# Moving the experts' weight loads and the last tiles' routing steps in a hand-written schedule (layers of scan, mixture of experts, attention and MLP, one Trainium2 core)

## The chip, the core and the metric

The kernel runs on 1 core of one Trainium2 (trn2) chip. The metric is the device time of one execution in microseconds (us). Five engines run their own instruction streams and meet at semaphores: TensorE (PE in the rows, PEld for its weight loads), VectorE (DVE), ScalarE (ACT), GpSimd (POOL) and SyncE (SP). SP computes nothing: it waits for semaphores and issues DMAs one after the other (SPq in the rows).

## What is computed

Input x is [2, 1024, 256] in f32, that is 2048 tokens of 256 channels. Four residual layers follow each other:

```
x = x + scan_layer(layernorm(x))      # state-space scan, 64 states per channel, sequential over 1024 tokens
x = x + moe(layernorm(x))             # 8 experts, top 2, capacity 640 tokens an expert
x = x + linear_attention(layernorm(x))
x = x + gated_mlp(layernorm(x))
```

The part that matters here is the end of the first and the beginning of the second. The scan layer ends per token with `(y + x*D_param) @ out_proj_w.T`, and its sum with x is the residual x1. The mixture layer begins with

```
probs = softmax(layernorm(x1) @ Wg)
gate_vals, expert_idx = top_k(probs, 2)
pos = running count of the tokens, in token order, that chose the same expert
dispatched = rows of layernorm(x1), laid out by (expert, pos), where pos < 640
h = relu(dispatched @ w1[e]);  out = h @ w2[e]
```

A token's place depends on all tokens before it, so the tiles are ranked in order. An expert's rows may come from any tile.

## The kernel before, in words

Tokens are cut into 16 tiles of 128 (tiles 0 to 15), and for the scan into 32 chunks of 64 (two chunks a tile). `prepare` makes the scan's inputs, `selective_scan` runs the scan and everything up to the dispatch of the tokens, `experts` the eight experts, `second_layer` the attention and the MLP.

The order of the work in `selective_scan` is one list of steps, made by the generator `scan_schedule`. Every engine walks through the same list and picks the steps in which it has a part; the order of the list is thus the order in every engine's queue, SP's too. Semaphores do the rest, so a step stands still on an engine while the step ahead of it waits.

For each group of 16 channels of a chunk ("stream"), PE makes the factors and inputs, ACT the exponentials, DVE one long scan instruction (L1161). Behind the scan of a chunk come:

- "y": PE multiplies the states by C (L945). "y_out": ACT copies the result to the tile y_raw (L1098).
- "y_sel", the pick: SP issues 4 DMAs of 16 KB each that gather the wanted partitions of y_raw into the tile y_sb (L867). It waits for the chunk's "y_out". The last chunk, 31, has no pick: PE selects its rows itself, by 4 products (L984).
- "yT": PE turns both chunks of the tile (L980 from y_sb, and L984), and waits for the pick to have landed. "yt": ACT copies them to y_t (L1107, L1108) and POOL adds the skip term (L1332). "proj", "proj2": PE multiplies by the output weights (L956). "resid": DVE adds the input (L1185, tile x1o), and SP stores the rows (L860, x1_d).

Routing goes by blocks of tiles: (0 to 3), (4 to 7), (8 to 11), then b3 = tiles 12 to 14 and b4 = tile 15 alone. The steps of a block are NORM (stats L1203, aggr L1208, the square root on ACT L1114, the reciprocal L1212, norm L1219, and a copy of the token numbers L1223), "turn" (PE transposes the normed rows, L1007), "turned" (ACT copies them to the tile r_xt, L1125), "score" (PE, the gate's weights, L1017), CHOOSE ("logit" L1227, "top" L1240, "index" L1245, "sub" L1248, "exp" on ACT L1132, "float" L1252, "hot" L1255, "ind" L1259), "rank" (PE counts by products with a triangle, L1030 to L1034), WEIGH (L1262 to L1268), SETTLE (L1272 to L1292; "slot" writes the tile slots), "count", and "scatter": POOL issues two indirect DMAs a tile that write the normed rows to their places in disp_d (L1339). ACT's L1116, right behind the square root of b4, is a load of the table for Exp and a small activation that brings it forward.

"load_experts" is one more step, of SP alone: when the last inputs of the scan are made it issues the loads of w1 and w2 of experts 0 and 1, 4 DMAs of 1 MB (L889), into the tile `shared`, which held the scan's factors until then. In the kernel before it stands in the list at the last stream step, that is ahead of the last residual of the loop, the last pick (chunk 30), and the whole tail.

Then SP waits for the stores of x1 and for all 32 scatters, and `experts` begins: SP loads the rows of experts 0 and 1 from disp_d (L1512, xd), then everything for the second layer (L1560, L1562); PE transposes the rows (L1400) and multiplies (L1412, L1424).

The two lines that hold the waits of which most is said later:

```
sp.wait_ge(sem("y_out"), c + 1)                       # the pick, on SP
pe.wait_ge(sem(f"y_sel{th}"), Y_SEL * (c + 1))        # "yT", on PE
```

Of the kernel before, what the change touches and what calls it, by code (L numbers as in the profile page):

```python
# [630 lines left out]
TOTAL = CHUNKS * GROUPS  # L631
# [9 lines left out]
ROUTED = ((0, 4), (4, 4), (8, 4), (12, 3), (15, 1))  # L641
# [3 lines left out]
CHOOSE = ("logit", "top", "index", "sub", "exp", "float", "hot", "ind")  # L645
WEIGH = ("sum", "inv", "gate")
SETTLE = ("pick", "where", "kept", "slot")


def router_steps(blk):  # L650

    n = ROUTED[blk][1]
    yield from ([(name,)] for name in NORM)
    for i in range(n):
        yield ([("mm", i - 1)] if i else []) + [("tr", i)]
        yield [("xt", i)]
    yield [("mm_last", n - 1)]
    yield from ([(name,)] for name in (*CHOOSE, *WEIGH, "rank", *SETTLE, "count"))
    for i in range(n):
        for j in range(2):  # L660
            yield [("scatter", i, j)]
# [7 lines left out]
def scan_schedule():  # L669

    routing, z, open_z, ending = [], 0, False, False

    def stamp(name, *args):
        nonlocal z, open_z
        if name in Z_WRITE:
            assert not open_z
            open_z = True
            return (name, *args, z)  # L680
        if name in Z_DONE:
            open_z, z = False, z + 1
            return (name, *args, z - 1)
        if name in ("mm", "proj2"):
            return (name, *args, z)
        return (name, *args)

    def advance(c=CHUNKS, j=5):
        if routing:
            blk, steps = routing[0]  # L690
            if any(name in Z_WRITE for name, *args in steps[0]) and (ending or open_z or j not in ((5,), (1, 3))[c % 2]):
                return
            for name, *args in steps.pop(0):
                yield stamp(name, blk, *args)
            if not steps:
                routing.pop(0)

    def finish(i, what):

        nonlocal ending  # L700
        if what == "yT":
            ending = True
        yield stamp(what, i)
        if what == "resid":
            ending = False
            if i + 2 < TILES:
                yield ("load_epilogue", i + 2)
            for b, (first, n) in enumerate(ROUTED[:-2]):
                if i == first + n - 1:
                    routing.append((b, list(router_steps(b))))  # L710

    for gi in range(TOTAL + LAG):
        c, j = divmod(gi, GROUPS)
        if gi < TOTAL:
            starts = j == 0 and c % CPB
            yield ("stream", gi)
            if starts:
                yield stamp("first_out", c)
        elif gi < TOTAL + LAG:
            yield ("scan", gi - LAG)  # L720
        yield from advance(c, j)
        if c >= CHUNKS - 4 and routing and not any(name in AT_PACE for name, *args in routing[0][1][0]):
            yield from advance(c, j)
        c_read, step = divmod(gi - LAG, GROUPS)
        c_read -= 1
        if 0 <= c_read < CHUNKS and step < len(Y_STEPS) and Y_STEPS[step]:
            yield ("y", c_read, Y_STEPS[step])
        for at, what in ((Y_OUT, "y_out"), (Y_PICK, "y_sel")):
            ended, rest = divmod(gi - LAG - GROUPS - at, GROUPS)
            if rest == 0 and 0 <= ended < CHUNKS - 1:  # L730
                yield (what, ended)
        for at, at_last, what in TILE_END:
            for i in range(TILES - 1):
                if gi == GROUPS * (CT * (i + 1)) + LAG + Y_OUT + (at if i < TILES - 2 else at_last):
                    yield from finish(i, what)
        if j == GROUPS - 1 and (c + 1) % CPB and c + 1 < CHUNKS:
            yield stamp("first", c + 1)
        if j < len(LOADS) and 1 <= c < CHUNKS - 1:
            yield ("load_parts", c + 1, j)
        if gi == GROUPS + 2:  # L740
            yield from (("load_epilogue", 0), ("load_weights",))
        if gi == 2 * GROUPS + 2:
            yield ("load_epilogue", 1)
        if j == GROUPS // 2 and 4 <= c < 4 + 2 * ZEROS:
            yield ("zero_slots", c - 4)
        if gi == TOTAL - 1:
            yield ("load_experts",)
    while routing:
        yield from advance()


    b3, b4 = len(ROUTED) - 2, len(ROUTED) - 1
    yield ("y_sel", CHUNKS - 2)
    yield from ((name, b3) for name in NORM)
    for js in (js for js in Y_STEPS if js):
        yield ("y", CHUNKS - 1, js)
    yield ("y_out", CHUNKS - 1)
    yield stamp("yT", TILES - 1)
    yield ("turn", b3)
    yield stamp("yt", TILES - 1)  # L760
    yield ("turned", b3)
    yield stamp("proj", TILES - 1)
    yield stamp("proj2", TILES - 1)
    yield from (("score", b3, i) for i in range(ROUTED[b3][1]))
    yield stamp("resid", TILES - 1)
    yield from ((name, b4) for name in NORM)
    yield from (("turn", b4), ("turned", b4), ("score", b4, 0))
    yield from ((name, b3) for name in CHOOSE)
    yield ("rank", b3)
    yield from ((name, b4) for name in CHOOSE[:-1])  # L770
    yield from ((name, b3) for name in WEIGH)
    yield from ((name, b3) for name in (*SETTLE, "count"))
    yield from (("scatter", b3, i, j) for i in range(ROUTED[b3][1]) for j in range(2))
    yield (CHOOSE[-1], b4)
    yield ("rank", b4)
    yield from ((name, b4) for name in (*WEIGH, *SETTLE))
    yield from (("scatter", b4, i, j) for i in range(ROUTED[b4][1]) for j in range(2))


def selective_scan(k, a, s):  # L780
    pe, act, dve, pool, sp, sem = k.pe, k.act, k.dve, k.pool, k.sp, k.sem
    ident, eps, slots = s["ident"], s["eps"], s["slots"]
    with ExitStack() as ctx:
# [29 lines left out]
        bank_in = [k.psum[:, 1024:2048], k.psum[:, 2048:3072]]  # L813
        bank_y, bank_z = k.banks[6], k.banks[7]
        schedule = list(scan_schedule())
        x1_at = {c: z + 1 for kind, *x in schedule if kind == "resid" for c, z in (x,)}
        u0_at = {c: z + 1 for kind, *x in schedule if kind == "first_out" for c, z in (x,)}
# [1187 lines left out]
```

## Time and profile before

| | us |
|---|---|
| 3 runs of the kernel before, median | 1322.31 |
| lowest and highest of the three | 1314.65, 1324.99 |
| the profiled execution, its own time | 1319.23 |
| its span, from first to last instruction | 1317.8 |
| mean granted clock of TensorE in it, as a share of full | 0.924 |
| busy: PE, DVE, ACT, POOL | 1105.0, 842.5, 503.4, 306.7 |

All rows come from the profiled execution; its own time is 1.4 us longer than its span. Times in the rows are counted from the start of the span. The scan ends at about 691 us, the dispatch lasts until about 727 us, the experts run from 732 to about 1025 us, and the second layer ends the span. The busy shares are averages over these very different stages.

### The profile page before, as it was taken

Reading aid. Unit: us, or ns where it says so; the run is one execution under the profiler, and the core shown is the slowest. Engines: PE = TensorE matmul, PEld = TensorE weight load, DVE = VectorE, ACT = ScalarE, POOL = GpSimd, SP = SyncE. Lnnn points to the kernel's source line nnn. Section 1 sums busy time; section 2 is a strip of 40 time slices with the busy share of each in tenths; the row PEclk is TensorE's granted clock in tenths of the full one; section 3 lists DMA queues with packets and bytes.
Section 4 is the critical chain, followed back from the end, with each engine's and each line's share of the span. In section 5 each row is a group of like instructions: output and inputs, shape, how many; then the busy total and the mean of one; then the engine's idle time right before and its main releaser. Section 6 shows DMA issues by size and latency. Waiting matters only on the chain.

```text
span 1317.8 us, 29499 instructions
## 1 busy us (share of the span) xinstructions
PE 1105.0 (84%) x11952; PEld 701.6 (53%) x11952; DVE 842.5 (64%) x1006; ACT 503.4 (38%) x1245; POOL 306.7 (23%) x930
## 2 busy tenths in 40 slices
PE   3647888878878898888873799999999588999998
PEld 2435444444544454444432578888887245475565
DVE  5858999999999999999992111111211577742211
ACT  3865556566656655566551111111111110122110
POOL 9741222222233222522242011111111200000000
PEclk9865789999999899999996799999999698999999
DMA  3897345543222222322223823222200400000000
GB/s 107 243 281 215 77 96 132 131 118 82 57 62 76 55 60 52 82 57 49 53 70 148 313 79 102 100 101 99 80 16 16 128 0 0 0 9 8 16 16 16
DMA packets 171687, 112.02 MB, mean 85 GB/s; under 512 B 93637, under 2 KB 162248, under 8 KB 169248
## 3 DMA queue, kind: packets, MB, share of 16 engines
q1 hardware_dynamic: 163120, 88.69, 24.2%
q0 software_dynamic: 8000, 20.87, 4.8%
q8 instruction: 94, 1.54, 0.5%
q10 hardware_dynamic: 432, 0.59, 0.2%
q14 instruction: 41, 0.34, 0.1%
HBM read 63.18 MB, written 45.90 MB: 83 GB/s over the span
## 4 chain that ended last, share of the span: by engine, by line
PE 47%; DVE 27%; issue 14%; SPq 5%; ACT 4%; DMA 2%; POOL 1%; DVEq 0%; ACTq 0%; POOLq 0%
DVE h L1161 19%; PE psum L1412 11%; PE psum L1424 11%; PE psum L1896 8%; PE psum L1907 4%; PE psum L945 3%; DVE den L1726 2%; PE psum L931 2%; PE psum L1852 2%; ACT decay L1046 1%; PE psum L912 1%; SPq L278 1%; SPq L199 1%; PE psum L1844 1%; SPq L282 1%
## 5 line engine op out<-in xcount | busy, mean ns | idle before, releaser
L1161 DVE TENSOR_TENSOR_SCAN h<-decay,psum 128x1024 f32<-128x1024 f32 x256 | 565.8, 2268 | 14.8 <-ACT psum L1056 9.0
L1046 ACT ACTIVATE decay<-psum 128x512 f32<-128x512 f32 x512 | 279.2, 600 | 200.5 <-PE psum L912 197.9
L931 PE MATMUL psum<-xdiag,bstat 96*128 96x64 bf16 x4096 | 176.4, 200 | 56.2 <-DVE h L1161 53.4
L931 PEld LDWEIGHTS psum<-xdiag,bstat 96*128 96x128 bf16 x4096 | 144.9, 102 | 82.0 <-DVE h L1161 73.5
L912 PEld LDWEIGHTS psum<-rows,shared 32*128 32x128 bf16 x4096 | 79.0, 96 | 183.4 <-issue 119.9
L945 PE MATMUL psum<-h,cstat 128*32 128x512 f32 x1024 | 150.2, 664 | 1.1 <-DVE h L1161 1.1
L1412 PE MATMUL psum<-xdt,shared 128*128 128x320 f32 x512 | 141.0, 436 | 0.7 <-ACT xdt L1471 0.7
L1424 PE MATMUL psum<-shared,hid 128*128 128x256 f32 x640 | 139.5, 379 | 0.6 <-ACT hid L1465 0.6
L1317 POOL TENSOR_TENSOR carry<-decay,h 128x16 f32<-128x16 f32 x240 | 57.9, 241 | 343.7 <-ACT decay L1046 343.4
L1424 PEld LDWEIGHTS psum<-shared,hid 128*128 128x128 f32 x640 | 121.0, 190 | 17.2 <-issue 1.1
L912 PE MATMUL psum<-rows,shared 32*128 32x64 bf16 x4096 | 110.5, 195 | 15.7 <-ACT decay L1046 7.4
L1412 PEld LDWEIGHTS psum<-xdt,shared 128*128 128x128 f32 x512 | 98.3, 192 | 41.4 <-issue 2.2
L1896 PE MATMUL psum<-xt,wgu 128*128 128x512 f32 x256 | 112.8, 600 | 2.5 <-DVE at L1731 2.5
L1499 DVE TENSOR_SCALAR hid<-psum 128x320 f32<-128x320 f32 x64 | 31.5, 492 | 112.2 <-PE psum L1412 112.2
L1534 POOL DMA_INDIRECT picked_d<-eo,to x40 | 39.0, 975 | 258.8 <-ACT eo L1468 133.5
L899 PE MATMUL psum<-r_tri 128*128 128x512 bf16 x222 | 67.8, 387 | 28.8 <-ACT decay L1046 27.5
L1502 DVE TENSOR_SCALAR eo<-psum,gate 128x256 f32<-128x256 f32 x20 | 9.7, 484 | 116.9 <-PE psum L1424 111.1
L1896 PEld LDWEIGHTS psum<-xt,wgu 128*128 128x128 f32 x256 | 49.1, 192 | 64.2 <-issue 59.4
L1749 DVE TENSOR_TENSOR shared<-psum,sil 128x512 f32<-128x512 f32 x32 | 22.1, 692 | 81.4 <-PE psum L1896 81.4
L1465 ACT ACTIVATE hid<-psum 128x320 f32<-128x320 f32 x64 | 28.0, 437 | 118.4 <-PE psum L1412 118.4
L1820 ACT ACTIVATE sil<-psum 128x512 f32<-128x512 f32 x32 | 19.1, 597 | 131.2 <-PE psum L1896 127.1
L1323 POOL TENSOR_TENSOR carry<-carry,u 128x16 f32<-128x16 f32 x240 | 52.8, 220 | 24.5 <-ACT u L1084 4.2
(201 smaller groups left out, 1100.9 us busy)
## 6 DMA issues: line engine op xcount, KB each, us to landing
shared<-in_w SPq DMA_DIRECT2D x16, 1024.0 KB, 4.8
xdiag<-x_parts_d SPq DMA_DIRECT2D x256, 48.0 KB
x_parts_d<-x_parts POOLq DMA_DIRECT2D x46, 256.0 KB, 7.8
parts_d<-dt_parts SPq DMA_DIRECT2D x24, 256.0 KB, 8.4
rows<-parts_d SPq DMA_DIRECT2D x128, 48.0 KB
disp_d<-zero SPq DMA_DIRECT2D x4, 1305.0 KB, 8.5
xd<-disp_d SPq DMA_DIRECT2D x8, 652.5 KB, 6.4
picked_d<-zero SPq DMA_DIRECT2D x4, 1024.0 KB, 5.2
```

The source lines that it names most:

```text
L899: pe.q.matmul(bank, tri[:, 1, :], tri[:, 1, :].unsqueeze(1).broadcast_to([P, 4, P]), start=True, stop=True)
L912: ins = pe.q.matmul(bank_a[half][:, i * T:(i + 1) * T], s["astat"][strip, RCH * g + q, :], rows[strip, c % 2, q, :], start=True, stop=True)
L931: ins = pe.q.matmul(to.rearrange("p d (s e) -> p s d e", e=2), bstat[0:ROWS, c % 2, b, :], xdiag[0:ROWS, c % 2, b, :, d, :], start=True, s ...
L945: ins = pe.q.matmul(bank_y[32 * q:32 * q + 32, :].rearrange("p (s d e) -> p s d e", s=2, e=4), s["cstat"][:, tok // 4, :], h[:, first:last ...
L1046: act.q.activation(decay[:, gi % NB, 8 * half:8 * half + 8, :], per_d(bank_a[half]), ACT.Exp).then_inc(sem("exp"), 1)
L1161: dve.q.tensor_tensor_scan(out=h[:, half_slot(c, half), ch:ch + G, :].rearrange("p d t -> p (d t)"), data0=decay[:, gi % NB, :, :].rearran ...
L1317: pool.q.tensor_tensor(whole, first, h[:, half_slot(c - 1, half), ch:ch + G, T - 1], ALU.mult).then_inc(sem("carry_made"), 1)
L1323: pool.q.tensor_tensor(whole.rearrange("p (h i) -> p h i", h=2), whole.rearrange("p (h i) -> p h i", h=2), own, ALU.add).then_inc(sem("car ...
L1412: ins = pe.q.matmul(table.bank(key)[:, 0:half_cap], w1[:, e % 2, dh, f * P:(f + 1) * P], xdt[:, e % 2, dh, c * half_cap:(c + 1) * half_cap ...
L1424: ins = pe.q.matmul(table.bank(key)[:, 0:D], hid[:, e % 2, f, st * P:(st + 1) * P], w2[:, e % 2, f, :], start=f == 0, stop=f == FT - 1)
L1896: ins = pe.q.matmul(table.bank(key)[:, :], wgu[:, j, dh, f * P:(f + 1) * P], xt[:, u, dh, :], start=dh == 0, stop=dh == 1)
L1907: ins = pe.q.matmul(table.bank(key)[:, 0:D], gt[:, blk % 2, f, n * P:(n + 1) * P], wd[:, f, :], start=f == 0, stop=f == FT - 1)
```

## The change

`load_experts` leaves the last stream step and is put behind the last pick, `y_sel` of chunk 30. In the tail, b3's turn goes ahead of tile 15's "yT", its scores ahead of tile 15's projection, and its CHOOSE (all but the exponential) and rank ahead of tile 15's residual and of b4's NORM. The exponential of b3 stands behind b4's NORM, and so behind the table load. All of b4's CHOOSE stands behind b3's scatter steps; before, all but its last step stood ahead of b3's WEIGH.

```diff
-        if gi == TOTAL - 1:
-            yield ("load_experts",)
     while routing:
         yield from advance()
 
 
     b3, b4 = len(ROUTED) - 2, len(ROUTED) - 1
     yield ("y_sel", CHUNKS - 2)
+    yield ("load_experts",)
     yield from ((name, b3) for name in NORM)
     for js in (js for js in Y_STEPS if js):
         yield ("y", CHUNKS - 1, js)
+    yield ("turn", b3)
     yield ("y_out", CHUNKS - 1)
+    yield ("turned", b3)
     yield stamp("yT", TILES - 1)
-    yield ("turn", b3)
     yield stamp("yt", TILES - 1)
-    yield ("turned", b3)
+    yield from (("score", b3, i) for i in range(ROUTED[b3][1]))
     yield stamp("proj", TILES - 1)
     yield stamp("proj2", TILES - 1)
-    yield from (("score", b3, i) for i in range(ROUTED[b3][1]))
+    yield from ((name, b3) for name in CHOOSE if name != "exp")
+    yield ("rank", b3)
     yield stamp("resid", TILES - 1)
     yield from ((name, b4) for name in NORM)
+    yield ("exp", b3)
     yield from (("turn", b4), ("turned", b4), ("score", b4, 0))
-    yield from ((name, b3) for name in CHOOSE)
-    yield ("rank", b3)
-    yield from ((name, b4) for name in CHOOSE[:-1])
-    yield from ((name, b3) for name in WEIGH)
-    yield from ((name, b3) for name in (*SETTLE, "count"))
+    yield from ((name, b3) for name in (*WEIGH, *SETTLE, "count"))
     yield from (("scatter", b3, i, j) for i in range(ROUTED[b3][1]) for j in range(2))
-    yield (CHOOSE[-1], b4)
+    yield from ((name, b4) for name in CHOOSE)
     yield ("rank", b4)
```

The two lines that go shift everything below them in the changed file, so that a line number there is 2 lower than in the kernel before (L867 is L865).

SP's queue at the end of the scan, in the kernel before. y_sb is the pick, shared<-in_w the experts' weights, x_d<-x1o the store of a tile's residual, xd<-disp_d the experts' rows:

```order
L867 DMA y_sb<-y_raw 32x128 x4
L889 DMA shared<-in_w 128x2048 x4
L860 DMA x_d<-x1o 128x256
L867 DMA y_sb<-y_raw 32x128 x4
L860 DMA x_d<-x1o 128x256
L1512 DMA xd<-disp_d 128x5x261 x2
```

The same place of SP's queue in the changed kernel:

```order
L865 DMA y_sb<-y_raw 32x128 x4
L858 DMA x_d<-x1o 128x256
L865 DMA y_sb<-y_raw 32x128 x4
L887 DMA shared<-in_w 128x2048 x4
L858 DMA x_d<-x1o 128x256
L1510 DMA xd<-disp_d 128x5x261 x2
```

The 4 weight loads have gone from ahead of tile 14's store and the last pick to behind both.

PE's queue behind the last states, in the kernel before (h,cstat is "y"; ident,y_sb and ident,y_raw are "yT"; ident,decay is "turn", since the normed rows of b3 and b4 lie in the tile decay; w_out,y_t the projection; r_wg,r_xt the scores; r_ind and r_before the rank):

```order
L945 MATMUL psum<-h,cstat 32x512 x20
L980 MATMUL psum<-ident,y_sb 128x128
L984 MATMUL psum<-ident,y_raw 128x32 x4
L1007 MATMUL psum<-ident,decay 128x128 x6
L956 MATMUL psum<-w_out,y_t 128x256 x2
L1017 MATMUL psum<-r_wg,r_xt 128x8 x6
L1007 MATMUL psum<-ident,decay 128x128 x2
L1017 MATMUL psum<-r_wg,r_xt 128x8 x2
L1030 MATMUL psum<-r_ind,r_tri 128x24
```

The same place of PE's queue in the changed kernel:

```order
L943 MATMUL psum<-h,cstat 32x512 x20
L1005 MATMUL psum<-ident,decay 128x128 x6
L978 MATMUL psum<-ident,y_sb 128x128
L982 MATMUL psum<-ident,y_raw 128x32 x4
L1015 MATMUL psum<-r_wg,r_xt 128x8 x6
L954 MATMUL psum<-w_out,y_t 128x256 x2
L1028 MATMUL psum<-r_ind,r_tri 128x24
L1030 MATMUL psum<-r_ind,r_tri 128x16
L1030 MATMUL psum<-r_ind,r_tri 128x8
L1032 MATMUL psum<-r_before,r_tri 128x24
L1005 MATMUL psum<-ident,decay 128x128 x2
L1015 MATMUL psum<-r_wg,r_xt 128x8 x2
```

The 6 transposes of b3 are now ahead of the wait for the pick, the 6 scores ahead of the projection, and b3's rank ahead of b4's transposes. On ACT, b3's three copies to r_xt stand ahead of the two to y_t, and its exponential is the first instruction behind the table load and its small activation. On DVE, b3's eight steps from L1227 to L1259 stand ahead of tile 15's residual and norm, and b4's stand behind b3's count. POOL's queue is the same. The number of instructions, of table loads and of DMAs is the same on every engine.

## Rows read from the trace of the kernel before

**Rows 1.** Chain of waits in order of time, 693 to 735 us: start us, us, what.

```profile
693.99 9.08 DMA y_sb<-y_raw
...
703.21 0.45 PE psum L980
...
708.44 0.43 DVE x1o L1185
...
709.89 1.28 ACT L1116
...
716.07 0.33 POOL disp_d L1339
...
725.06 2.46 DMA disp_d<-decay,slots
...
727.89 4.11 DMA xd<-disp_d
...
732.05 2.20 PE psum L1400 x9
```

**Rows 2.** Timeline of SP's queue: start us, us, engine, line, op, out<-in, count.

```profile
687.84 2.09 SPq L889 DMA_DIRECT2D shared<-in_w  x4
691.75 0.33 SPq L860 DMA_DIRECT2D x_d<-x1o  x1
692.17 2.44 SPq L867 DMA_DIRECT2D y_sb<-y_raw  x4
...
728.88 0.52 SPq L1560 DMA_DIRECT2D x<-x_d  x1
```

**Rows 3.** DMA issues of two stretches: count, KB each, us to landing.

```profile
x_d<-x1o SPq DMA_DIRECT2D x1, 128.0 KB, 1.7
...
skip_c<-skip_d SPq DMA_DIRECT2D x1, 128.0 KB, 2.6
```

**Rows 4.** Stretches: us, busy PE, PEld, DVE, ACT, POOL, clock, DMA share, GB/s.

```profile
696.00:697.00 1.00, 0.00 (x0) 0.00 (x0) 0.00 (x0) 0.00 (x0) 0.00 (x0) 1.00 1.10 460
698.00:699.00 1.00, 0.00 (x0) 0.00 (x0) 0.00 (x0) 0.00 (x0) 0.00 (x0) 0.50 1.01 426
701.00:702.00 1.00, 0.00 (x0) 0.00 (x0) 0.00 (x0) 0.00 (x0) 0.00 (x0) 0.50 0.57 182
...
738.00:740.00 2.00, 2.00 (x8) 1.37 (x7) 0.49 (x1) 0.05 (x1) 0.00 (x0) 0.80 1.12 370
```

**Rows 5.** Timeline of the engines, 688 to 717 us, columns as in rows 2.

```profile
688.28 1.13 PE L956 MATMUL psum<-w_out,y_t 128*128 128x256 f32 x4 [0.53 <-POOL y_t L1332]
691.46 3.64 PE L945 MATMUL psum<-h,cstat 128*32 128x512 f32 x32 [1.05 <-DVE h L1161]
695.17 0.77 ACT L1098 COPY y_raw<-psum 128x128 f32<-128x128 f32 x4 [1.65 <-PE psum L945]
...
705.01 1.52 PE L1007 MATMUL psum<-ident,decay 128*128 128x128 f32 x6
706.53 1.87 PE L956 MATMUL psum<-w_out,y_t 128*128 128x256 f32 x4
708.24 1.40 PE L1017 MATMUL psum<-r_wg,r_xt 128*128 128x8 f32 x12
...
705.24 0.27 ACT L1107 COPY y_t<-psum 128x128 f32<-128x128 f32 x1 [9.29 <-PE psum L984]
706.57 0.92 ACT L1125 COPY r_xt<-psum 128x256 f32<-128x256 f32 x3 [0.90 <-PE psum L1007]
711.29 0.35 ACT L1125 COPY r_xt<-psum 128x256 f32<-128x256 f32 x1
...
710.49 0.17 DVE L1227 COPY r_logit<-psum 128x24 f32<-128x24 f32 x1
712.03 0.18 DVE L1259 TENSOR_TENSOR r_ind<-r_hot 128x24 bf16<-128x24 f32 x1
713.73 0.17 DVE L1262 TENSOR_REDUCE r_total<-r_prob 128x3 f32<-128x24 f32 x1
```

## The prediction

> **What bounds the kernel now.** I read the page first (its busy shares mix stages, so they decide nothing here), then the chain of waits in order of time around the end of the scan, then SP's queue and the stretches of the same time, then the timeline of the engines for the prices. In the chain [rows 1] the reader is to see four pieces. From 693.99 us the chain is a DMA, the last pick, for 9.08 us: it lands at 703.07 and PE starts "yT" at 703.21. From there to 716.07 it runs through PE, ACT and DVE in many small steps: tile 15's residual, its norm, and both blocks' choosing. From 716.07 to 725.06 it is POOL, that issues the eight scatters of b3 and b4. Then fixed latencies: 2.46 us until the last scatter has landed, the issue of the experts' rows at 727.89, 4.11 us until they are there, and PE begins the experts at 732.05. Nothing else is on the chain between 694 and 732, so a microsecond saved ahead of the first scatter is one saved in the whole, if nothing replaces it.
>
> Why does a pick of 4 times 16 KB take 9 us? SP's queue [rows 2] shows it: the four 1 MB loads were issued from 687.84, the pick from 692.17 to 694.61. The DMA engines are full (1.10 and 1.01 of their time, 460 and 426 GB/s at 696 and 698) and run out of work between 701 and 702, with 182 GB/s left [rows 4]. The small transfers got through only when the big ones ended. Meanwhile PE does nothing, and its granted clock, still 1.00 at 696, is 0.50 at 698 and at 701 (1.2 instead of 2.4 GHz) [rows 4]; so "yT" begins at half clock.
>
> **The change, part by part.** The sum follows the changed order from the end of "y", which it leaves where it is: PE's last L945 ends at 695.10 and ACT's copy to y_raw at 695.94 [rows 5].
>
> *The loads behind the pick.* SP waits for tile 14's residual as before and issues its store at 691.75, the pick from 692.17 [rows 2]. The four loads come behind it, from 694.6. The last of the pick's four issues begins at 693.99 [rows 1]. The trace has no pick whose landing is told and that stands free; the nearest transfers land 1.7 and 2.6 us after issue, with 128 KB each [rows 3]. So the pick is there between 695.7 and 696.6; I take 2.1 us, 696.1, in the middle. At the other end it lands no earlier than now, 703.07: that is a rival below.
>
> *Turn and "yT".* The 6 transposes took 1.52 us at half clock [rows 5]; the clock is full at that time [rows 4], so about 0.8: 695.15 to 695.95, in the time in which PE would wait for ACT and the pick anyway. They need b3's norm, which DVE made during "y". "yT" took 703.21 to 705.2 [rows 1, 5], the second of these being just ahead of ACT's copy at 705.24, at half clock; at full 1.0: 696.1 to 697.1. ACT now makes b3's three copies first, 0.92 us from 696.0 [rows 5], so to 696.95, and is free when "yT" ends. From "yT" to the start of the projection it was 705.2 to 706.53, 1.3 us over ACT and POOL: the projection can start at 698.4.
>
> *Scores ahead of the projection.* 12 passes in 1.40 us [rows 5], from 697.1, when both PE and the copies are ready: 698.5. The scores cost the projection 0.1 us only, since they run while ACT and POOL make y_t. The projection took 1.13 us at full and 1.87 at half clock [rows 5]; it ends at 699.6 or 700.4.
>
> *Choosing ahead of the residual.* From L1227 to the end of L1259 it is 710.49 to 712.21, 1.72 us [rows 5]: 698.53 to 700.25. The residual can then start at 700.28, and it would have been ready at 699.65: choosing delays tile 15's chain by some 0.6 us, and takes its own 1.72 off the end of it.
>
> *Residual to exponential.* From 708.44 [rows 1] to the first activation behind the table load at 711.29 [rows 5] it is 2.85 us, the load's 1.28 among them [rows 1]. The exponential of b3 is that activation now: 703.13. It lasts some 0.22 us, so DVE begins to weigh at 703.37. Before, b3's exponential stood behind b4's copy; now b4's copy stands behind it, 0.2 us late, which nobody needs yet.
>
> *Weighing, settling, first scatter.* From 713.73 [rows 5] to 716.07 [rows 1], 2.34 us, the same instructions and the same handing over to POOL: 705.71. Eight starts as far apart as before, 8.99 us [rows 1]: the last at 714.70. The last scatter begins 10.4 us earlier than the 725.06 of before. It needs b4's slots: all the choosing and weighing of both blocks and b4's last steps lay behind 710.49 and ended before 717, 6.5 us; even if b4 alone took all of it behind b3's count at about 705.2, its slots would stand at 711.7, and the seventh scatter (705.71 plus six of the 1.28 us between starts) comes at 713.4. So b4's choosing, moved behind b3's, is covered by POOL, with 1.7 us or more to spare.
>
> *The stretch behind it* moves as a whole. The weights: 4.2 MB at 426 GB/s [rows 4] are 9.8 us, from about 695.4, so there at 705.2, at the slow end of the stretches around 707; tile 15's store, issued at about 700.7, is queued behind them and lands by then too. SP asks for it at about 717. The experts' rows and everything behind start 10.4 us earlier, with TensorE's clock at half as now: PE has stood 16 us by 732 and has the clock back in the stretch 738 to 740 [rows 1, 4]; it will have stood nearly as long.
>
> Sum: 7.1 us from "yT" starting at 696.1 instead of 703.2, and 3.3 from the shorter way from there to the first scatter (9.6 instead of 12.9 us). 10.4 us off the profiled execution's 1319.23 is 1308.8; off the median of the three runs, 1322.31, it is 1311.9. The mean of those four executions is 1320.3, and I take 1310.
>
> Bounds of the gain: "yT" can't start before the turn and the copy to y_raw are done, 695.95, so with full clock and the pick at 695.7 it is 10.6. With half clock throughout (turn +0.7, "yT" +1.0, and scores and their copies late by half a microsecond) and the pick at 696.6, the weighing starts some 2.3 us later: 8.1. I keep 8 to 11.
>
> The row of the table load is that of two, 1.28 us, and the next activation starts directly behind it [rows 1, 5]. The Trainium skill (ScalarE: Activation LUTs, section What ACT_TABLE_LOAD costs) says that a switch costs a drain of 1.38 us on top, 2.66 in all. By that page the exponential, which now hangs directly on the load, would come 1.4 us later and the time would be 1311.4; the trace does not show such a drain, and the sum goes by the row.
>
> **Rivals.**
>
> *The pick is slow whatever stands ahead (a).* If the 16 engines serve small and big transfers that overlap alike, the pick could still land only with the weights, now issued directly behind it, at about 705.2. Turn would be early, but scores stand behind "yT" on PE, so all waits: 705.2 plus the 9.6 us from there to the first scatter is 714.8 instead of 716.07. Gain 1.3 us, time 1319. For it: the pick issued behind the weights waited 9 us. Against it: the experts' rows landed in 4.11 us although 2 MB more was issued 1 us behind them, at 728.88 [rows 1, 2]; what stands ahead wasn't held back.
>
> *Weights beside the routing (b).* The loads now run from 695 to 705, the time in which all engines route, where before they ran beside idle ones. If copies, the table load or tile 15's store suffer, say a quarter more on the 9 us from 696.1 to 705.1, 2.2 us are given back, and if the first scatters are slowed, 2 more: gain 6 to 8, time about 1313. Against it: from 688 to 696, while the loads already ran, PE went through the projection (1.13 us) and "y" (3.64 us), and ACT through its four copies (0.77 us), each back to back [rows 5].
>
> *Clock at the experts' start (c).* If PE's shorter rest left the clock at full, the 6.4 us at half from 732.05 to about 738.4 would be worth 3.2 more: gain 13.6, time 1306. Against it: PE rested from 695.1 and the clock was at half by 698 [rows 4, 5]; the rest ahead of the experts stays near 15 us.
>
> *b4 too late (d), slower.* b4's choosing behind b3's count is the one thing that gets later. It decides once its slots come behind 713.4, where the seventh scatter would start; every microsecond beyond costs one. To be at the old time they would have to come 10.4 us behind that, at 723.8, and to be 13.2 us slower than that at 737. That would be a time from 1332 on. I find 711.7 at the worst.
>
> **How the numbers follow.** Main case 0.70, (a) 0.08, (b) 0.12, (c) 0.07, (d) 0.03. One per cent, 13.2 us, is about what a measurement of this kernel can tell from no change. The forecast gain is 0.8%, inside it. The three runs lie 10 us apart, so a true 10.4 may come out above 13.2, in the main case about one time in four (0.18), and in (c) most often (0.05): 0.23 faster. (d) gives 0.03 slower. The rest, 0.74, is within 1%. The runs' lowest less 11 is 1303.6, their highest less 8 is 1317; with (b) and (c) inside and some of (a) the range is 1303 to 1318.
>
> **What would show it.** After the change: the pick's DMA no longer in the chain, PE's idle time ahead of "yT" under 1 us, transposes of b3 between "y" and "yT", first scatter near 705.7 and the last near 714.7, PE's first L1400 transpose (now L1398) near 721.7, weights running beside the routing. The forecast is wrong if PE still waits for the pick over 2 us (a), if any DVE or ACT step of the stretch is longer than in [rows 5] (b), if the clock is full at the experts' start (c), if POOL pauses between sixth and seventh scatter (d), or if the stages from the experts on change their length by more than a microsecond or two.

## The result, and the profile after

The changed kernel took 1312.39 us in the median of 20 runs (1307.70 to 1320.50), the kernel before 1321.91 (20 runs, 1314.65 to 1328.20). The ratio is 0.9935, with a 95% interval of 0.9918 to 0.9951: by the ratio 8.6 us less, 6.5 to 10.8 (the medians lie 9.5 us apart). The forecast was 1310 (1303 to 1318), a gain of 10.4 us. The profiled execution of the changed kernel took 1313.42 us, its span is 1311.9.

The chain of waits in order of time around the end of the scan, in the changed kernel; it answers to [rows 1] (line numbers are 2 lower than before, so L1183 is the residual, L1337 the scatter, L1398 the experts' transposes):

```profile
697.80 0.81 PE psum L1005 x6
698.60 0.22 PE psum L978
698.82 0.95 PE psum L982 x8
699.78 1.36 PE psum L1015 x12
...
702.89 0.44 DVE x1o L1183
...
704.34 1.28 ACT L1114
...
708.33 0.33 POOL disp_d L1337
...
717.35 2.46 DMA disp_d<-decay,slots
...
720.20 4.12 DMA xd<-disp_d
...
724.37 2.19 PE psum L1398 x9
...
727.42 20.30 PE psum L1410 x64
```

The DMA of 9.08 us that began the chain in [rows 1] is gone: "y" hands over to b3's transposes, these to "yT", with no rest. What is left is PE, DVE and ACT in a row, then POOL's eight scatters, then the same two latencies as before.

SP's queue, answering to [rows 2]:

```profile
694.45 0.33 SPq L858 DMA_DIRECT2D x_d<-x1o  x1
694.87 2.37 SPq L865 DMA_DIRECT2D y_sb<-y_raw  x4
697.28 2.26 SPq L887 DMA_DIRECT2D shared<-in_w  x4
703.34 0.33 SPq L858 DMA_DIRECT2D x_d<-x1o  x1
```

The pick goes out first, the four loads directly behind it. The scan itself ended 2.7 us later in this execution than in the one of before, so absolute times can't be compared. The useful zero is the end of PE's last product of "y", at 695.10 before and 697.80 after. No step of PE, ACT, DVE or POOL ahead of it was moved. The loads were, and they ran beside the last scans before; but the table of the experiments shows no sign of that in the scan's end (with all loads ahead 693.2 to 696.4, with all behind 691.1 to 698.1). The timeline of the engines, answering to [rows 5]:

```profile
694.16 3.64 PE L943 MATMUL psum<-h,cstat 128*32 128x512 f32 x32 [1.55 <-DVE h L1159]
697.73 0.87 PE L1005 MATMUL psum<-ident,decay 128*128 128x128 f32 x6
698.52 0.30 PE L978 MATMUL psum<-ident,y_sb 128*128 128x128 f32 x1
698.69 1.09 PE L982 MATMUL psum<-ident,y_raw 128*128 128x32 f32 x8
699.62 1.50 PE L1015 MATMUL psum<-r_wg,r_xt 128*128 128x8 f32 x12
701.10 1.13 PE L954 MATMUL psum<-w_out,y_t 128*128 128x256 f32 x4
...
705.63 0.20 ACT L1114 ACTIVATE r_warm<-eps 128x1 f32<-128x1 f32 x1
705.74 0.21 ACT L1130 ACTIVATE r_prob<-r_less 128x24 f32<-128x24 f32 x1
...
705.98 0.18 DVE L1260 TENSOR_REDUCE r_total<-r_prob 128x3 f32<-128x24 f32 x1 [0.95 <-ACT r_prob L1130]
...
710.19 0.15 DVE L1290 TENSOR_TENSOR slots<-r_at,r_over 128x2 uint32<-128x2 f32 x1
...
716.06 0.98 POOL L1337 DMA_INDIRECT disp_d<-decay,slots  x1 [0.30 <-issue]
```

"yT" and the projection run at full clock (1.13 us, against 1.87 in [rows 5]). b4's slots are written at 710.34, and the seventh scatter, the first that needs them, starts at 716.06: 5.7 us to spare. The stretches, answering to [rows 4] (us, busy PE, PEld, DVE, ACT, POOL, clock, DMA share, GB/s):

```profile
699.00:701.00 2.00, 2.00 (x19) 2.00 (x18) 0.00 (x0) 1.00 (x5) 0.67 (x1) 1.00 0.77 319
701.00:703.00 2.00, 1.29 (x8) 0.76 (x8) 1.70 (x15) 0.00 (x0) 0.05 (x1) 0.86 1.06 446
703.00:705.00 2.00, 0.23 (x4) 0.12 (x4) 1.53 (x6) 0.96 (x2) 0.00 (x0) 0.50 0.97 410
...
732.00:734.00 2.00, 2.00 (x7) 1.37 (x6) 0.49 (x1) 0.23 (x1) 0.00 (x0) 0.71 1.03 398
```

The weights now run beside the routing. The clock falls in the changed kernel too, but late: it is 1.00 until 701, 0.86 in the 2 us in which the projection ends (702.23), and 0.50 behind. And at the experts' start it came back only between 732 and 734, some 8.8 us behind PE's first transpose, where it had been some 6.8 us before.

### The profile page after: what moved, and what is told of

It is laid out like the page before. It is cut to its first block, busy times and chain, and to the rows that moved or that the text cites. A ratio compares the mean times of both kernels' runs of the same rounds, so it can differ in the third digit from the quotient of the medians.

```text
span 1311.9 us, 29499 instructions
## 1 busy us (share of the span) xinstructions
PE 1111.4 (85%) x11952; PEld 703.2 (54%) x11952; DVE 842.6 (64%) x1006; ACT 503.0 (38%) x1245; POOL 307.0 (23%) x930
## 4 chain that ended last, share of the span: by engine, by line
PE 48%; DVE 28%; issue 13%; SPq 4%; ACT 4%; DMA 2%; POOL 1%; DVEq 0%; ACTq 0%; POOLq 0%
DVE h L1159 20%; PE psum L1410 11%; PE psum L1422 11%; PE psum L1894 8%; PE psum L1905 4%; PE psum L943 3%; PE psum L929 2%; DVE den L1724 2%; PE psum L1850 2%; ACT decay L1044 2%; PE psum L910 2%; SPq L278 1%; SPq L199 1%; PE psum L1842 1%; SPq L282 1%
```

## The experiments

One table first. Every trace was read at the same marks, in us from the end of "y" (the first column says when that was). "Rest" is from PE's first transpose of the experts' rows to the end of the span. The two kernels stand twice, since each was run and traced again. The ratios below are against the kernel before timed in the same session, whose median was 1321.51 us for e1 to e4, 1317.41 for e5 and the repeated kernels, and 1319.81 for e6 and e7.

| trace | end of "y" | "yT" starts | first scatter | last scatter | PE's first transpose | rest |
|---|---|---|---|---|---|---|
| before | 695.1 | 8.11 | 20.97 | 29.96 | 36.95 | 585.8 |
| before, again | 693.2 | 7.65 | 20.57 | 29.59 | 36.81 | 585.9 |
| changed | 697.8 | 0.72 | 10.53 | 19.55 | 26.57 | 587.5 |
| changed, again | 691.3 | 0.72 | 10.52 | 19.54 | 26.65 | 586.0 |
| e1, loads only | 698.1 | 0.72 | 12.10 | 21.09 | 28.43 | 585.5 |
| e2, order only | 696.4 | 7.78 | 19.67 | 28.66 | 35.94 | 585.6 |
| e7, half the loads ahead | 688.5 | 4.40 | 16.29 | 25.31 | 32.51 | 586.9 |
| e4, loads last | 697.6 | 0.64 | 10.52 | 19.52 | 27.50 | 586.4 |
| e3, weigh first | 694.7 | 0.74 | 7.36 | 16.38 | 23.47 | 585.6 |
| e3, again | 691.1 | 0.72 | 7.35 | 16.33 | 23.57 | 585.6 |
| e5, 8 products | 696.6 | 0.73 | 7.35 | 16.35 | 23.53 | 584.2 |
| e6, 11 products | 695.4 | 0.73 | 7.35 | 16.36 | 23.44 | 581.5 |

For one and the same kernel the columns between repeat to 0.5 us or better, the first moves by up to 6.5 us and the last by up to 1.5: a good reason to judge a change of this size by marks inside the trace and use the times only to confirm it.

### Only the loads moved (e1)

```diff
 # to the kernel before
-        if gi == TOTAL - 1:
-            yield ("load_experts",)
...
     yield ("y_sel", CHUNKS - 2)
+    yield ("load_experts",)
```

> Only the experts' weight loads are moved behind the last pick; the order of the tail is that of the kernel before. All times from the end of PE's last product of y to POOL's first scatter of b3: 20.97 us in the kernel before, 10.53 us in the changed one. Theory (the queue held the pick, and the new order only shortens the way behind it): the pick has landed when the copy to y_raw is done, PE starts yT within 1 us of the end of y, and the first scatter comes at 12 us, since the old order then pays for b4's norm and both blocks' choosing in a row; gain over before about 9 us (ratio 0.993). Rival (the new order is what saved the time, because b3's turn and scores run in the wait): first scatter at 18 us or more, gain 3 us or less.

Measured: 1312.34 us (12 runs), ratio 0.9923 (0.9898 to 0.9948). The first scatter came at 12.10. Two rows of its chain and one of PE's timeline:

```profile
696.92 1.74 DMA y_sb<-y_raw
...
698.80 0.30 PE psum L979
```

```profile
698.80 0.30 PE L979 MATMUL psum<-ident,y_sb 128*128 128x128 f32 x1 [0.72 <-DMA y_sb<-y_raw]
```

With no weights ahead the pick lands 1.74 us after its last issue instead of 9.08, although four 1 MB loads were issued right behind it. The two never moved at the same time: the pick's 128 packets of 512 bytes had ended by 698.37, and the first packet of the loads began at 698.77. In the kernel before they ran from 701.0 to 702.2, while the loads' last packets ran until 701.7. 20.97 to 12.10 is 8.9 us: this one edit is most of the 10.4 us by which the first scatter comes earlier in the changed kernel.

### Only the order (e2)

```diff
 # to the changed kernel
+        if gi == TOTAL - 1:
+            yield ("load_experts",)
...
     yield ("y_sel", CHUNKS - 2)
-    yield ("load_experts",)
```

> Only the order of the tail is the new one; the loads stay ahead of the last pick. Theory: PE still waits for the pick until about 8 us behind the end of y, scores stand behind yT on PE and so wait too; only turn, the three copies and the shorter way behind the residual are saved: first scatter at 19 us (20.97 before), gain about 2 us (ratio 0.9985). Rival (the new order is what saved the time): first scatter at 13 us or less, gain 7 us or more.

Measured: 1319.37 us (12 runs), ratio 0.9985 (0.9963 to 1.0008), which can't be told from nothing; the marks can, 20.97 to 19.67, 1.3 us. PE's rows:

```profile
704.13 0.45 PE L979 MATMUL psum<-ident,y_sb 128*128 128x128 f32 x1 [6.98 <-DMA y_sb<-y_raw]
704.37 1.75 PE L983 MATMUL psum<-ident,y_raw 128*128 128x32 f32 x8
705.93 2.71 PE L1016 MATMUL psum<-r_wg,r_xt 128*128 128x8 f32 x12
708.49 2.05 PE L955 MATMUL psum<-w_out,y_t 128*128 128x256 f32 x4
```

PE waits 6.98 us (8.11 before; b3's transposes now fill 0.9 of it), and its clock falls: it is 0.50 from 701.3 on, until 738.9. The 12 passes of the scores take 2.71 us instead of 1.50, the projection 2.05 instead of 1.13. From "yT" to the first scatter it is 11.89 us here and 9.81 in the changed kernel, with the same instructions: the rest costs its own length and then 2.1 us more. The loads do not explain this difference, since here they have ended and there they still run.

### Half the loads ahead (e7)

```diff
 # to the changed kernel
+        if gi == TOTAL - 1:
+            yield ("load_experts", 0)
...
-    yield ("load_experts",)
+    yield ("load_experts", 1)
...
                 elif kind == "load_experts":
                     sp.wait_ge(sem("inputs"), TOTAL)
-                    for e in range(2):
+                    for e in x:
```

> The changed kernel's order; the two loads of expert 0 (2 MB) are issued ahead of the last pick as before, the two of expert 1 behind it. Theory (the pick waits for the bytes ahead of it in the queue): 2 MB at 426 GB/s are 4.9 us less than all four, so yT starts some 2.9 us behind the end of y (7.78 with four ahead, 0.72 with none), and the first scatter at 12.5 to 13.5 us (19.67 and 10.53). Rival (any big load issued near the pick holds it, ahead or behind): yT starts 6 us or more behind the end of y.

One run, 1309.35 us. The pick in its chain, and PE's start:

```profile
687.41 5.38 DMA y_sb<-y_raw
```

```profile
692.92 0.45 PE L980 MATMUL psum<-ident,y_sb 128*128 128x128 f32 x1 [3.59 <-DMA y_sb<-y_raw]
```

The last issue to landing is 1.74 us with no weights ahead, 5.38 with 2 MB, 9.08 with 4 MB (8.61 and 8.79 in the two other traces with 4 MB ahead). So the pick is later the more bytes stand ahead of it, but the number was missed: "yT" at 4.40, not 2.9. The packets of the trace show where. The first two loads went out at 681.20, and 104 of the pick's 128 packets had run by 690.05, 1.5 us behind the end of "y", in time for the forecast; the other 24 ran in three groups of eight until 691.85, beside packets of the next loads. The pick landed at 692.79. Why these 24 were late is not shown: the trace doesn't say which DMA engine moved a packet. My reading is that three of the engines were behind the others with their share of the loads, and that a transfer has landed when its last engine is done. The even steps of 3.6 and 3.7 us are thus no rate: the first holds the 1.8 us of the late packets. The first scatter was missed by more (16.29, not 13.5), since the clock fell within the 3.59 us of rest and "yT" began at half clock: from "yT" it is 11.89 us, as in e2.

### Loads behind the last residual (e4)

```diff
 # to the changed kernel
     yield ("y_sel", CHUNKS - 2)
-    yield ("load_experts",)
...
     yield stamp("resid", TILES - 1)
+    yield ("load_experts",)
```

> The changed kernel with the experts' loads behind the last residual's store: they are issued about 6 us behind the end of y instead of beside it, and run beside the scatters instead of beside the routing. Theory (DMA traffic beside the routing cost nothing): the routing steps from yT to the first scatter take the same time within 0.3 us as in the changed kernel (9.8 us from L978 to L1337), the weights have landed before the experts' rows are there, and the time is that of the changed kernel. Rival (loads beside the routing cost something): the routing gets shorter by 1 us or more. Second rival (loads beside scatters are worse): the last scatter or the experts' rows land 2 us or more later than the changed kernel's 2.46 and 4.12 us, and the time is 2 us or more above it.

Measured: 1310.57 us (9 runs), ratio 0.9916 (0.9886 to 0.9947), not to be told from the changed kernel. The routing, from L978 to the first scatter, took 9.88 us, against 9.81. SP issued the loads from 703.54, and their packets ran from 704.6 to 718.4, so they left the first 6.3 us of the routing and were beside its last 3.5 in both kernels. That the weights beside these first 6.3 us cost nothing is shown; for most of the last 3.5 it rests on the rows of weighing and settling, 2.35 us in the changed kernel (705.98 to 708.33) against 2.34 in [rows 5] and [rows 1], where no weights ran. One stretch of e4, and its chain at the end of the scatters:

```profile
707.00:709.00 2.00, 0.23 (x3) 0.14 (x3) 1.76 (x16) 0.21 (x1) 0.85 (x1) 0.50 0.98 410
```

```profile
717.15 3.30 DMA disp_d<-decay,slots
...
720.83 4.26 DMA xd<-disp_d
```

The last scatter lands after 3.30 us instead of 2.46 with the weights still running, and PE begins 0.9 us later. So beside the routing, where the change put them, the loads cost nothing that shows; beside the scatters they cost a little. That is under the 2 us of the second rival, and too little for the times to show.

### b3 weighed and scattered first (e3)

```diff
 # to the changed kernel
-    yield from ((name, b3) for name in CHOOSE if name != "exp")
+    yield from ((name, b3) for name in CHOOSE)
     yield ("rank", b3)
+    yield from ((name, b3) for name in (*WEIGH, *SETTLE))
+    yield from (("scatter", b3, i, j) for i in range(ROUTED[b3][1]) for j in range(2))
     yield stamp("resid", TILES - 1)
     yield from ((name, b4) for name in NORM)
-    yield ("exp", b3)
     yield from (("turn", b4), ("turned", b4), ("score", b4, 0))
-    yield from ((name, b3) for name in (*WEIGH, *SETTLE, "count"))
-    yield from (("scatter", b3, i, j) for i in range(ROUTED[b3][1]) for j in range(2))
+    yield ("count", b3)
```

> The changed kernel, and b3 goes on without a stop: its exponential, weighing, settling and scatters stand ahead of tile 15's residual and of b4's norm. Theory (POOL's eight issues, 1.28 us apart, are the bound once the first can start, and tile 15's chain fits into the first six): the first scatter comes 7.3 us behind the end of y instead of 10.5, the last 9.0 us behind the first; gain over before about 11.5 to 13.5 us (ratio 0.991). It needs two more loads of ACT's tables, 1.28 us each, one ahead of b3's exponential and one ahead of b4's root. Rival (b4 gets late, since its residual waits for b3's whole choosing and for the table loads): POOL pauses by 2 us or more ahead of the seventh scatter, and the gain is that of the changed kernel, 8 to 10 us.

> The kernel of e3 once more, for a closer time and a second trace. Theory: the way from the end of y to PE's first transpose of the experts is 23.5 us again (36.95 before, 26.57 in the changed kernel), and the time is 12 to 14 us under that of before, 2 to 4 under the changed kernel. Rival (the 14 us of its first timing were luck, and something behind gives time back): gain under 11 us.

Measured: 1305.64 us (6 runs), ratio 0.9894 (0.9856 to 0.9932), and again 1303.82 us (6 runs), ratio 0.9893 (0.9870 to 0.9916). POOL's scatters and the slots of b4 in the first trace:

```profile
702.07 0.99 POOL L1337 DMA_INDIRECT disp_d<-decay,slots  x1 [4.10 <-DVE slots L1290]
...
708.51 0.98 POOL L1337 DMA_INDIRECT disp_d<-decay,slots  x1 [0.30 <-issue]
709.80 0.98 POOL L1337 DMA_INDIRECT disp_d<-decay,slots  x1 [0.30 <-issue]
711.09 0.98 POOL L1337 DMA_INDIRECT disp_d<-decay,slots  x1 [0.30 <-issue]
```

```profile
708.01 0.15 DVE L1290 TENSOR_TENSOR slots<-r_at,r_over 128x2 uint32<-128x2 f32 x1
```

No pause ahead of the seventh: b4's slots stand at 708.16, 1.6 us before it starts. The first scatter is at 7.36, as forecast to a tenth. Tile 15's chain, from its residual at 701.22 to its slots, is done before the six scatters of b3 are. The two added table loads (697.18 and 699.50) fell into waits of ACT: each had ended 0.8 us or more before DVE had the next input ready. It beats both kernels by the marks: 13.5 us on the way against before, 3.1 against the changed kernel. The times give 14.0 and 14.1 us against before, at the upper end of the forecasts or a little over; against the changed kernel the intervals overlap, so there the marks alone tell.

### PE kept busy until the rows land (e5, e6)

```diff
 # to e3's kernel, behind b4's rank on PE; 8 in e5, 11 in e6
+                    if blk == len(ROUTED) - 1:
+                        pe.wait_ge(sem("z_free"), x1_at[TILES - 1])
+                        for _ in range(11):
+                            pe.q.matmul(bank_z, ident[:, :], ident[:, :].unsqueeze(1).broadcast_to([P, 4, P]),
+                                        start=True, stop=True)
```

> The kernel of e3, and behind b4's rank PE runs 8 products of the identity with itself into a free PSUM bank (128x512, f32, two passes each), some 11 us at the clock that it has, that is about as long as it would stand until the experts' rows are there; their result is not used. Theory (the experts' first 6.4 us or more at half clock cost about 3 us): the clock is full when the rows arrive, the ten first transposes take 1.3 us instead of 2.4 and the 64 passes behind them 17.3 instead of 19.2; time about 3 us under e3's. Rival (products beyond the wait delay the transposes, or DMA and scatters suffer): PE starts the transposes over 0.5 us behind the landing of the rows, or the last scatter comes later than 16.4 us behind the end of y, and less than 1.5 us is won.

> The kernel of e5 with 11 products instead of 8. In e5 they ended at 717.3, PE then stood 2.8 us, the ten transposes ran at full clock in 1.32 us, but the clock fell to half at about 722, and only 1.4 us was won behind the first transpose (584.2 us from there to the end instead of 585.6). Theory (what counts is that PE stands nowhere for long before the rows land): 3 more products take 2.6 us at full clock and end within 0.5 us of the landing; transposes 1.3 us, the 64 passes 17.3 to 17.8 us, 582.5 us from the first transpose to the end, gain over before 15 us or more (ratio 0.987). Rival (PE's few steps between transposes and passes, where it waits for copies, are rest enough, or the clock falls anyhow): the 64 passes take 18.5 us or more again.

These measure the price in the third rival, the clock at the experts' start. PE's rows of e5, and the stretches in which its clock fell:

```profile
720.15 1.32 PE L1403 MATMUL psum<-ident,xd 128*128 128x128 f32 x10 [2.81 <-DMA xd<-disp_d]
722.24 18.98 PE L1415 MATMUL psum<-xdt,shared 128*128 128x320 f32 x64 [0.77 <-ACT xdt L1474]
```

```profile
720.00:722.00 2.00, 1.32 (x10) 1.08 (x10) 0.75 (x5) 1.13 (x2) 0.00 (x0) 0.97 1.10 356
722.00:724.00 2.00, 1.76 (x4) 1.20 (x5) 0.56 (x5) 0.00 (x0) 0.00 (x0) 0.50 1.10 349
```

PE's rows of e6:

```profile
707.62 11.07 PE L1037 MATMUL psum<-ident 128*128 128x512 f32 x22
718.83 1.31 PE L1403 MATMUL psum<-ident,xd 128*128 128x128 f32 x10
720.91 17.47 PE L1415 MATMUL psum<-xdt,shared 128*128 128x320 f32 x64 [0.77 <-ACT xdt L1474]
```

and those of e3's second trace:

```profile
714.70 2.40 PE L1398 MATMUL psum<-ident,xd 128*128 128x128 f32 x10 [11.20 <-DMA xd<-disp_d]
717.76 19.22 PE L1410 MATMUL psum<-xdt,shared 128*128 128x320 f32 x64 [0.66 <-ACT xdt L1469]
```

With 8 products PE rested 2.8 us ahead of the rows; the transposes ran at full clock, but then the clock fell for a while (the 64 passes took 18.98 us), and 1.4 us was won instead of 3. With 11 the rest was gone and the clock stayed full: the end of the passes came 2.7 us earlier, counted from the first transpose (19.55 us against 22.28). The whole rest of the program was 4.1 us shorter; the other 1.4 us lie in the second layer, where the clock's rises moved too, and are not shown to be the products' doing. Times: e5 1304.44 us, ratio 0.9888 (0.9864 to 0.9911); e6 1302.01 us, ratio 0.9878 (0.9850 to 0.9906). The 1.4 us of e5 don't show in its time: e3, timed beside it, took 1303.82. The forecast for e6 was 0.987; its interval overlaps with e3's, so that e6 is the fastest of all is shown by the marks, not by the times.

### Both kernels once more

> The changed kernel once more, for a second trace. Theory (the local gain is fixed and the rest of the difference is chance): the way from the end of y to PE's first transpose is 26.6 us again within 0.2; the moment of the end of y, 697.8, and the stretch from the first transpose to the end, 587.5 us (585.8 before), differ from the first trace by one or two us. Rival (the change itself gives time back behind): both stay at 697.8 and 587.5 within 0.3 us.

> The kernel before once more, for a second trace. Theory: the way from the end of y to PE's first transpose of the experts is 36.95 us again within 0.3, the end of y moves by one or two us from 695.1, and the stretch behind is 585.8 within 2 us. Rival (the way itself varies by 2 us or more from run to run): it does here.

The changed kernel again: 1308.14 us (6 runs), ratio 0.9923 (0.9901 to 0.9945). Its first transposes, and the passes:

```profile
717.90 2.40 PE L1398 MATMUL psum<-ident,xd 128*128 128x128 f32 x10 [15.20 <-DMA xd<-disp_d]
720.96 19.46 PE L1410 MATMUL psum<-xdt,shared 128*128 128x320 f32 x64 [0.66 <-ACT xdt L1469]
```

The kernel before again: 1318.42 us (10 runs), ratio to itself 1.0007 (0.9988 to 1.0027). The way from the end of "y" to PE's first transpose was 36.95 and 36.81 us before, 26.57 and 26.65 after: 10.3 us less, with 0.1 us of play. The end of "y" moved from 697.8 to 691.3 in one and the same kernel, and the rest from 587.5 to 586.0. So the 2.7 us by which the scan ended later in the first trace, and the 1.8 us by which its rest was longer (1.0 of them in the first 64 passes, 20.30 against 19.28 us, while the clock came back late), are chance and not the change's doing: in the second pair they are -1.9 and 0.1 us.

## Why the prediction was right

The wait. The step "small transfers got through only when the big ones ended" held: e1 shows it by putting the loads behind the pick, and e7, which halves them, gives a landing in between, though not the forecast one. The pick's landing was put at 2.1 us after its last issue, and measured at 1.74 in e1. In the changed kernel "yT" started at 0.72 (forecast 1.0), behind b3's transposes and not behind the pick.

The way to the first scatter. It was forecast step by step at 10.6 us behind the end of "y", and came at 10.53. The residual was forecast 5.2 us behind the end of "y" and came at 5.1, b3's exponential 8.0 and 7.9. The step that was right in size but left two causes in one is the 3.3 us "from the shorter way": the experiments split it. In the old order the way from "yT" is 12.86 us behind a rest (before) and 11.38 without (e1), in the new order 11.89 (e2) and 9.81 (changed). So of the 3.05 us 1.5 to 2.1 are the clock and 1.0 to 1.6 the order, by which of the two one takes first. In all twelve traces "yT" began at full clock where PE had stood 0.72 us or less ahead of it, and at half where it had stood 3.59 us or more. The clock's share differs since the kernel before had it back at 708 and did its scores at full (1.40 us, as in e1), while e2 did them at half (2.71). The prediction had both in its terms ("yT" 1.0 instead of 2.0, the projection at full clock), but called them one thing. Its lower bound has a term too small: "half clock throughout" made the scores and their copies late by half a microsecond, where e2's scores alone are 1.2 us longer than at full clock. That did not touch the forecast, since the clock stayed full up to the projection.

The scatters and behind. Eight issues in 9.02 us (8.99 before), 2.46 and 4.12 us of latency: the stretch moved as a whole, and PE began 26.57 us behind the end of "y", against 26.6 by the forecast.

The size. The marks give 10.4 and 10.3 us, the times 8.6 (6.5 to 10.8) in the first comparison and 10.1 (7.2 to 13.0) in the second. The difference between 8.6 and 10.4 is inside the interval; no step is needed to explain it. That 1312.39 lies so near 1310 is partly luck, since executions of one kernel lie over 10 us apart; the marks are the better witness. The second pair of traces shows that the surplus of the first one behind PE's first transpose went away by itself.

The table load. The row of the changed kernel decides between the trace and the Trainium skill (ScalarE: Activation LUTs, section What ACT_TABLE_LOAD costs): the load starts at 704.34, the small activation at 705.63, b3's exponential at 705.74. No drain of 1.38 us shows here. In e3's first trace the load ahead of b3's exponential ends at 698.46 and the exponential starts at 699.26, waiting for DVE, and the small activation behind the last load starts 0.01 us behind it (703.95, 703.96). The load between these can't tell, since the activation behind it waits 1.58 us for DVE.

The rivals. The slow pick (a) did not come: in e1 and the changed kernel the loads issued right behind the pick did not hold it. But there the pick had ended before the loads' first packet, so these two don't test its premise, that small and big transfers in flight together share the engines alike. Where they did overlap, in e7, 24 of 128 packets came up to 1.8 us late, and not at the end of the loads. Weights beside the routing (b): 9.88 us with the first 6.3 free of them (e4), 9.81 with them throughout, where the rival wanted 2.2 more; refuted. The clock at the experts' start (c) did not come by itself: it was at half for 8.8 and 7.1 us behind the first transpose (6.7 and 7.0 before). Its price is 2.7 us in the stage (e6), where 3.2 was written. b4 too late (d): 5.7 us to spare, even 1.6 in e3.

## What to carry to other kernels

Look at the order of SP's queue as an order of its own. Here a small transfer that the next step waited for landed some 7 us sooner after its issue once it was issued ahead of large ones that were wanted much later, and the large ones cost nothing that shows beside the routing's short steps. A wait on TensorE can cost more than its length, since what follows may run at half clock (here 7.4 us of wait and 1.5 to 2.1 us behind it). And when steps are reordered, look for the engine whose fixed row of issues ends the stage, here POOL's eight scatters of 1.28 us, and bring its first item forward; e3 shows how much other work can run beneath it, with 1.6 us to spare.

## What the runs showed of the hardware that was not expected

- Landing time against bytes ahead in the queue: 1.74 us for none, 5.38 for 2 MB, 8.61 to 9.08 for 4 MB. With 2 MB ahead and 2 MB behind, 24 of the pick's 128 packets ran up to 1.8 us later than the others.
- PE at rest for 2.8 us (e5) kept its clock through the ten transposes that followed, and lost it 1.7 us after they had begun; at rest for 3.59 us (e7) it had lost it before "yT", and the scores behind ran at half clock (2.71 us instead of 1.50). In the changed kernel it fell at 702.4, 0.2 us behind the projection, although PE had worked from 694.16 to 702.23 without a rest that shows.
- The same program ended its scan at 697.8 us in one execution and at 691.3 in another, while the 27 us behind that repeated to 0.1 us.
